# Layer 2 sampling of a four-layer convolution kernel: placings as two column tiles, convolution mid-chunk, bias by halves, far hats sent first

## The reference, cut to what matters

```
def bilinear_gather(x, py, px):
    y0, x0 = floor(py), floor(px);  wy, wx = py - y0, px - x0
    corners = [(y0, x0, (1-wy)*(1-wx)), (y0, x0+1, (1-wy)*wx), (y0+1, x0, wy*(1-wx)), (y0+1, x0+1, wy*wx)]
    return sum(x[corner] * weight * valid for each corner)            # (B, C, 9, H, W)
def deform_conv(x, offset, w, b):
    py, px = base_y + dy, base_x + dx                                 # 9 taps, own offsets per pixel
    return einsum('bckhw,ock->bohw', bilinear_gather(x, py, px), w) + b
s0 = deform_conv(x, conv3x3(x, off_w0, off_b0), dw0, db0)
s1 = deform_conv(x, conv3x3(x, off_w1, off_b1), dw1, db1)
wts = softmax(...mean of s0 and s1...);  fused = wts[0] * s0 + wts[1] * s1
return fused + conv1x1(x, cr_w, cr_b) * gate
```

## Time and profile before

| | |
|---|---|
| median of 3 runs | 1371.48 us (1370.13 to 1371.91) |
| profiled execution, its own time | 1369.67 us |
| its span in the trace | 1367.9 us |
| PE (TensorE matmul) busy | 1123.3 us, 82% of the span |
| DVE (VectorE) busy | 889.0 us, 65% |
| POOL (GpSimd) busy | 663.8 us, 49% |
| ACT (ScalarE) busy | 641.7 us, 47% |
| stage `windows1` | about 383 to 769 us |
| all spreads L1604 | x1296 matmuls, 100.6 us busy |
| all samples L1623 | x1536 matmuls, 166.3 us busy |
| all convolution matmuls L1635 | x1728, 75.7 us busy |

### The profile page before, as it was taken

The page is one execution under the profiler, slowest core; times in us unless marked ns, Lnnn a source line. Parts: engine busy times, 40 slices in busy tenths (PEclk is TensorE's granted clock), DMA queues, the critical chain, the costliest instruction groups (busy, mean ns, idle before and its releaser), DMA issues. The chain is left out here.

```text
span 1367.9 us, 31420 instructions
## 1 busy us (share of the span) xinstructions
PE 1123.3 (82%) x13256; PEld 607.0 (44%) x13256; DVE 889.0 (65%) x1220; ACT 641.7 (47%) x1096; POOL 663.8 (49%) x503
## 2 busy tenths in 40 slices
PE   3970189878749999999999487799999999998658
PEld 2440077753316666666666343233333333334323
DVE  3788945566956666666666368646666676666623
ACT  1646025353636666666666443144444444445310
POOL 2000011103336676677665430188888888888500
PEclk9985599988859999999999787699999999999769
DMA  4100000001244555555544005000000000001002
GB/s 86 23 1 0 0 3 3 2 18 36 53 129 144 145 162 163 151 148 161 163 148 133 2 1 139 1 1 2 1 2 1 2 1 2 2 10 71 1 18 71
DMA packets 41840, 75.13 MB, mean 55 GB/s; under 512 B 20876, under 2 KB 26093, under 8 KB 40925
## 3 DMA queue, kind: packets, MB, share of 16 engines
q1 hardware_dynamic: 41533, 72.77, 19.0%
q10 hardware_dynamic: 160, 0.30, 0.1%
HBM read 60.73 MB, written 9.33 MB: 51 GB/s over the span
## 5 line engine op out<-in xcount | busy, mean ns | idle before, releaser
L2246 POOL TENSOR_TENSOR arena_sb<-arena_sb 128x768 f32<-128x768 f32 x168 | 323.4, 1925 | 120.5 <-ACT arena_sb L2207 99.8
L2207 ACT ACTIVATE arena_sb<-ps 128x768 f32<-128x768 f32 x216 | 174.8, 810 | 243.4 <-PE ps L2136 241.3
L2261 DVE TENSOR_REDUCE arena_sb<-ps 128x4 f32<-128x1536 f32 x108 | 188.9, 1758 | 127.7 <-PE ps L2103 126.2
L2136 PE MATMUL ps<-arena_sb 33*64 33x384 f32 x1728 | 187.4, 502 | 11.5 <-ACT arena_sb L2207 5.5
L1623 PE MATMUL ps<-arena_sb 120*64 120x216 f32 x1536 | 166.3, 355 | 9.7 <-DVE arena_sb L1745 9.7
L2148 PE MATMUL ps<-arena_sb 64*64 64x384 f32 x1728 | 168.1, 488 | 3.4 <-ACT arena_sb L2214 3.4
L1623 PEld LDWEIGHTS ps<-arena_sb 120*64 120x64 f32 x1536 | 104.2, 136 | 61.2 <-issue 21.9
L1685 ACT ACTIVATE xp_sb<-ps 128x432 f32<-128x432 f32 x192 | 101.9, 531 | 51.2 <-PE ps L1623 47.9
L2103 PE MATMUL ps<-arena_sb 32*128 32x384 f32 x864 | 113.4, 600 | 12.6 <-DVE arena_sb L2261 6.6
L1767 POOL TENSOR_SCALAR xp_sb<-xp_sb 128x384 f32<-128x384 f32 x69 | 102.9, 1492 | 39.7 <-PE ps L1604 28.5
L1739 DVE TENSOR_TENSOR arena_sb<-ps,arena_sb 120x384 f32<-120x384 f32 x216 | 119.5, 553 | 1.1
(11 more groups left out here) (249 smaller groups left out, 1655.8 us busy)
## 6 DMA issues: line engine op xcount, KB each, us to landing
xn_sb<-far_hats SPq DMA_DIRECT2D x96, 270.0 KB
arena_sb<-far_hats SPq DMA_DIRECT2D x48, 270.0 KB
arena_sb<-pixel_major SPq DMA_DIRECT2D x96, 120.0 KB, 4.4
far_hats<-xp_sb SPq DMA_DIRECT2D x24, 162.0 KB
pixel_major<-arena_sb SPq DMA_DIRECT2D x24, 108.0 KB
x_sb<-in_x SPq DMA_DIRECT2D x4, 576.0 KB, 8.4
arena_sb<-arena_sb SPq DMA_DIRECT2D x8, 288.0 KB, 5.6
xn_sb<-in_W SPq DMA_DIRECT2D x1, 2304.0 KB, 8.9
```

The lines of the kernel that those rows point to most:

```text
L2136: mm = pe.matmul(p_scores(g)[64 * i:64 * i + 64, h, :], kp[own, key:key + 64], qp[own, PIX * b2 + CH * ib:PIX * b2 + CH * ib + CH], start= ...
L2207: act.activation(pt[g % SLOTS].rearrange("p (h n) -> p h n", h=2), p_scores(g), ACT.Exp)\
L2246: pool.tensor_tensor(acc, first, pt[g % SLOTS], ALU.add).then_inc(S["pool_added"], 1)
L2261: v.tensor_reduce(part.rearrange("p (a u j) -> p a u j", a=3, u=NB)[:, a, :, jc], p_m(m), AX.X, ALU.max)\
```

## The change

- A placing is issued as two matmuls of 64 columns each, one for each column half of the array, the form of the samples.
- The groups are rearranged: spreads 0, 1 / 2, 3 / 4 / 5, 6 / 7, 8, samples 0, 1 / 2, 3 / none / 4, 5 / 6, 7, placings (far, 0, 1, 2) in groups 0, 1, 3 and 4, always between spreads and samples. Group 2 has the convolution behind its one spread.
- The convolution in the middle of chunk n computes the upper half of chunk n and the lower half of chunk n - 1 (whose samples 4 to 7 are still there). The first computes one half, and a last one behind the last chunk the other half of chunk 23.
- The bias is split by halves: ScalarE takes the upper half of both banks, VectorE the lower half of both, each signalling after every bank. The two turns behind a convolution wait each for its own bank.
- VectorE's bias stands between weights 4 and 5 of the next chunk.
- SyncE sends the far hats of chunk 0 (store and three reloads) ahead of the windows of chunks 0 and 1.

```diff
@@ -1495,6 +1495,7 @@
     pq = [ps[:, 512 * (6 + i):512 * (6 + i) + 512] for i in range(2)]
     pc = [ps[:, 512 * (6 + v):512 * (6 + v) + CH // 2] for v in range(2)]
     S4 = smp.rearrange("p (s y x) -> p s y x", s=TAPS, y=ROWS)
+    scf = sc.rearrange("p h n -> p (h n)")
     size = SLOTS * CH // 2
     hat = [[k["xn"][:, size * (2 * i + part):size * (2 * i + part) + size].bitcast(mybir.dt.float16)
             .rearrange("p (q n) -> p q n", q=SLOTS) for part in range(2)] for i in range(2)]
@@ -1502,29 +1503,26 @@
     far = temp[0:FAR, SLOTS, :]
     far_dram = k["far"]
 
-    def steps_of(i):
-
-        return range(2 * i, min(2 * i + 2, STEPS))
-
-    def tail(n, i):
-
-        return n + 2 < NQ and i < SLOTS
-
-    def head(n, i):
-
-        return n + 2 < NQ and i == SLOTS
-
-    ORDER = (SLOTS,) + tuple(range(SLOTS))
-    turn_of = {("place", 0, q): at for at, q in enumerate(ORDER)}
+    def halves(n):
+
+        return range(0 if n < NQ else 1, 2 if n else 1)
+
+    SPREADS = ((0, 1), (2, 3), (4,), (5, 6), (7, 8))
+    SAMPLES = ((0, 1), (2, 3), (), (4, 5), (6, 7))
+    MIDDLE = 2
+    ORDER = {0: SLOTS, 1: 0, 3: 1, 4: 2}
+    turn_of = {("place", 0, q): at for at, q in enumerate(ORDER.values())}
     for n in range(-1, NQ):
         for i in range(GROUPS):
-            if head(n, i):
+            if n + 2 < NQ and i != MIDDLE:
                 turn_of["place", n + 2, ORDER[i]] = len(turn_of)
-            if n >= 0 and 2 * i < PAIRS:
-                turn_of["sample", n, 2 * i] = len(turn_of)
-                turn_of["sample", n, 2 * i + 1] = len(turn_of)
-            if tail(n, i):
-                turn_of["place", n + 2, ORDER[i]] = len(turn_of)
+            if n >= 0:
+                for j in SAMPLES[i]:
+                    turn_of["sample", n, j] = len(turn_of)
+    after_conv = {}
+    for n in range(NQ):
+        first = min(turn_of["sample", n, 4], turn_of.get(("place", n + 2, ORDER[3]), len(turn_of)))
+        after_conv[first], after_conv[first + 1] = n + 1, n + 1
 
     with nc.Block() as block:
         @block.sync
@@ -1562,11 +1560,11 @@
                     sp.dma_start(xd[blk][KW // 2 * a:KW // 2 * (a + 1), :],
                                  src.unsqueeze(0).to_broadcast([WH, IW, BLOCK * CH])).then_inc(S[f"far_in{blk}"], 16)
 
-            window(0)
-            window(1)
             far_away(0)
             for blk in range(3):
                 far_back(0, blk)
+            window(0)
+            window(1)
             for n in range(-1, NQ):
                 if n >= 1 and n + 1 < NQ:
                     window(n + 1)
@@ -1580,12 +1578,17 @@
             def empty(u):
                 if u >= 2:
                     pe.wait_ge(S["emptied"], u - 1)
+                if u in after_conv:
+                    pe.wait_ge(S[f"sc{u % 2}"], 2 * after_conv[u] - 1)
 
             def place(m, q):
                 u = turn_of["place", m, q]
                 empty(u)
-                pe.matmul(pq[u % 2][:, 0:CH], k["selp"][:, q, :], o3[:, CH * m:CH * m + CH], start=True, stop=True)\
-                    .then_inc(S["filled"], 1)
+                for h in range(2):
+                    own = slice(64 * h, 64 * h + 64)
+                    mm = pe.matmul(pq[u % 2][own, 0:CH], k["selp"][:, q, own], o3[:, CH * m:CH * m + CH],
+                                   start=True, stop=True, skip_group_check=True)
+                mm.then_inc(S["filled"], 1)
 
             def spread(m, t):
                 g = m * STEPS + t
@@ -1609,9 +1612,6 @@
                 if i == 0:
                     pe.wait_ge(S["weights"], (n + 1) * STEPS)
                     pe.wait_ge(S[f"loaded{n % 2}"], 64 * (n // 2 + 1))
-                    if n:
-                        pe.wait_ge(S["sc0"], n)
-                        pe.wait_ge(S["sc1"], n)
                 u = turn_of["sample", n, i]
                 empty(u)
                 band, pair = divmod(i, NTX // 2)
@@ -1626,32 +1626,34 @@
                 mm.then_inc(S["filled"], 1)
 
             def conv(n):
-                pe.wait_ge(S["emptied"], turn_of["sample", n, PAIRS - 1] + 1)
+                last = ("sample", n, 3) if n < NQ else ("sample", n - 1, PAIRS - 1)
+                pe.wait_ge(S["emptied"], turn_of[last] + 1)
                 for t in range(TAPS):
                     for v in range(2):
                         own = slice(64 * v, 64 * v + 64)
-                        for h in range(2):
+                        for h in halves(n):
                             at = CH * t + CH // 2 * h
                             mm = pe.matmul(pc[v][64 * h:64 * h + 64, :], k["dws"][own, t, :], smp[own, at:at + CH // 2],
                                            start=(t == 0), stop=(t == TAPS - 1), skip_group_check=True)
                 mm.then_inc(S["conv"], 1)
 
-            for q in ORDER:
+            for q in ORDER.values():
                 place(0, q)
             for n in range(-1, NQ):
                 for i in range(GROUPS):
                     if n + 1 < NQ:
-                        for t in steps_of(i):
+                        for t in SPREADS[i]:
                             spread(n + 1, t)
-                    if head(n, i):
+                    if i == MIDDLE:
+                        if n >= 0:
+                            conv(n)
+                        continue
+                    if n + 2 < NQ:
                         place(n + 2, ORDER[i])
-                    if n >= 0 and 2 * i < PAIRS:
-                        sample(n, 2 * i)
-                        sample(n, 2 * i + 1)
-                    if tail(n, i):
-                        place(n + 2, ORDER[i])
-                if n >= 0:
-                    conv(n)
+                    if n >= 0:
+                        for j in SAMPLES[i]:
+                            sample(n, j)
+            conv(NQ)
 
         @block.scalar
         def _(act):
@@ -1680,7 +1682,9 @@
                 u = turn_of["sample", n, i]
                 band, pair = divmod(i, NTX // 2)
                 act.wait_ge(S["filled"], u + 1)
-                if i == 0 and n:
+                if band and not pair:
+                    act.wait_ge(S["conv"], n + 1)
+                elif n and not pair:
                     act.wait_ge(S["conv"], n)
                 act.activation(S4[:, :, IH * band:IH * band + IH, 2 * IW * pair:2 * IW * pair + 2 * IW],
                                pq[u % 2][:, 0:TAPS * IH * 2 * IW].rearrange("p (s y x) -> p s y x", s=TAPS, y=IH), ACT.Copy)\
@@ -1688,29 +1692,26 @@
 
             def biased(n):
                 act.wait_ge(S["conv"], n + 1)
-                for h in range(2):
-                    at = CH * n + CH // 2 * h
-                    last = act.activation(sc.rearrange("p h n -> p (h n)")[0:64, at:at + CH // 2],
-                                          pc[0][64 * h:64 * h + 64, :], ACT.Identity,
-                                          bias=k["dbs"][64 * h:64 * h + 64, 1:2])
-                last.then_inc(S["sc0"], 1)
-
-            for q in ORDER:
+                for v in range(2):
+                    act.activation(scf[64 * v:64 * v + 64, CH * n:CH * n + CH // 2], pc[v][0:64, :], ACT.Identity,
+                                   bias=k["dbs"][0:64, 1 + v:2 + v]).then_inc(S[f"sc{v}"], 1)
+
+            for q in ORDER.values():
                 magnitude(0, q)
             for n in range(-1, NQ):
                 for i in range(GROUPS):
                     if n + 1 < NQ:
-                        for t in steps_of(i):
+                        for t in SPREADS[i]:
                             keep_x(n + 1, t)
-                    if head(n, i):
+                    if i == MIDDLE:
+                        if n >= 0:
+                            biased(n)
+                        continue
+                    if n + 2 < NQ:
                         magnitude(n + 2, ORDER[i])
-                    if n >= 0 and 2 * i < PAIRS:
-                        keep(n, 2 * i)
-                        keep(n, 2 * i + 1)
-                    if tail(n, i):
-                        magnitude(n + 2, ORDER[i])
-                if n >= 0:
-                    biased(n)
+                    if n >= 0:
+                        for j in SAMPLES[i]:
+                            keep(n, j)
 
         @block.vector
         def _(v_):
@@ -1740,18 +1741,18 @@
 
             def biased(n):
                 v_.wait_ge(S["conv"], n + 1)
-                for h in range(2):
-                    at = CH * n + CH // 2 * h
-                    last = v_.tensor_scalar(sc.rearrange("p h n -> p (h n)")[64:128, at:at + CH // 2],
-                                            pc[1][64 * h:64 * h + 64, :], k["dbs"][64 * h:64 * h + 64, 2:3], None, ALU.add)
-                last.then_inc(S["sc1"], 1)
+                for v in range(2):
+                    v_.tensor_scalar(scf[64 * v:64 * v + 64, CH * n - CH // 2:CH * n], pc[v][64:128, :],
```

(13 more changed lines are left out.)

## The result

The changed kernel takes 1376.25 us, the median of 6 runs (1372.66 to 1378.64), against 1370.31 for the kernel before in 6 runs (1367.71 to 1371.91), the three of the table above and three more. The ratio is 1.0046, 95% interval 1.0031 to 1.0061: slower by about 6 us. Forecast were 8.7 us more, 1380.2. The direction held, and so did the mechanism, the hold of the second sample. Two terms of the sum were off: the order of the groups costs 4.6 us and not 9.7, and the start gives back 1.6 and not 2.8. The two errors point in opposite directions and partly cancel, so the number is nearer than its terms are.

A forecast was written before the change was run, and what follows sets the result against it. TensorE's in-order stream was taken to set the pace. Order of groups +9.7, start -2.8 and end +1.8 make +8.7 us: profiled execution 1378.4, median of runs 1380.2, own range 1375 to 1385, whole range 1370 to 1387.

The forecast's parts named there:

- the hold of the second sample: After a placing, the second sample waits for ScalarE to evict the placing's bank, 1.97 us after the spreads.
- the order of the groups: Placings between spreads and samples in four groups: chunk 15.54 against 15.10 us, +0.44 for each of 22 chunks, +9.7 us.
- the start: Far hats sent first in the lead-in: first reload 3.6 us earlier, partly lost at chunk 1's reload; -2.8 us.
- The column tiles: Placing as two tiles takes 0.19 us, hidden in the gap before the held sample: cost 0, upper end 0.15 per placing.
- rival B: No change: the cheaper way from placing into samples (0.19 for 0.27) pays for most of the hold; 1373 us; 9 in 100.
- The split bias: Bias by halves behind the convolution removes the 0.39 us wait; worth up to 0.46 alone, but eaten in this kernel.
- the eviction queue: ScalarE's biases, copies and placing eviction behind the convolution: late next, at +2.33 us, making that group 3.21 us.
- VectorE and GpSimd: VectorE's later biases and weights, and GpSimd's hat slots, are each covered by 0.4 us in a chunk: no cost.
- The cover: GpSimd's slot 2 ends about 8.5 us after the convolution, the spread needing it starts at 8.91: 0.4 us spare.
- The end: Last weight made later, so GpSimd's normalization ends later; extra half convolution of about 3.1 us runs beside it; +1.8 us.
- A: Rival, faster: second sample not held, bias wait gone; rounds of 2.59, chunk 14.9, 1366 us; 13 in 100.
- C: Rival, slower still: two-tile placing takes more than the free 0.39 us, or slot 2's cover is gone; 1389 to 1393; 8 in 100.

The follow-up runs named there:

- full: The kernel after with the placing back as one matmul over 128 columns, all else as changed; ratio to before 1.0061.
- cols: The kernel before with only the placings as two column tiles, in their old places; ratio to before 0.9987.
- hats: The kernel before with only the far hats of chunk 0 sent ahead of the windows; ratio to before 1.0005.
- bias_hats: The kernel before with the bias split by halves and the far hats of chunk 0 first; ratio to before 0.9933.
- bias_hats_w: The kernel before with bias by halves, far hats first, and the windows of chunk 1 sent behind chunk 1's far hats; ratio to before 0.9897.
- all4: As bias_hats_w, with the placings also as two column tiles in their old places; ratio to before 0.991.
- ahead: The kernel after with the placings of groups 0, 1 and 4 ahead of the spreads, on TensorE and in ScalarE's evictions; ratio to before 0.998.

## Why the prediction was right, point by point

**The order of the groups (forecast +0.44 a chunk, measured +0.21).** Right in each piece but one. Group 3: 3.21 forecast, 3.21 measured. Lone spread 0.70 and convolution 3.08: the same. The three other groups: 2.85 forecast, 2.77 measured; this term was mis-sized by 0.08, three times a chunk, 5 us in all. I took the whole distance of 1.97 from today's group 3. There the spreads stand behind a placing, and ScalarE's copies start 0.65 after them, because ScalarE must first take that placing out:

```profile
538.16 0.48 ACT L1670 ACTIVATE xp_sb<-ps 128x384 f32<-128x384 f32 x1
```

In after they stand behind a sample, and the copies start 526.22 - 525.64 = 0.58 after them; the placing's eviction takes 0.50 instead of 0.53, and from copies to eviction it is 0.76 instead of 0.74. The kernel before already shows the first: the lone spread at 540.73, also behind a sample, has its copy at 541.31, 0.58 after it. I read the row of the right operation in the wrong neighbourhood. With the 0.58 alone the chunk would have been forecast at 15.33.

**The column tiles (0, upper end +0.15 a placing).** Right. From placing to sample it is 0.19 where nothing is waited for (526.43 to 526.62), the value I took, and the price is hidden: `full` has the same chunk. The Trainium skill ("TensorEngine Tiling (Array Packing)", "Key Properties") says that a change of tiling mode drains TensorE. The runs agree in kind: 0.27 to 0.29 where the shape of the tile changes behind a placing, 0.18 to 0.19 where it does not. The saving that rival B drew from it is not there: `cols` gains 0.04 a chunk and `full` loses nothing. In this kernel spreads lie on one side of a placing and samples on the other, so one of its two sides changes shape in either form.

**The split bias (worth up to 0.46, eaten by the eviction queue).** Right, and shown apart: 0.37 alone, and in after the second sample at +2.33 behind the convolution, as forecast.

**VectorE and GpSimd (no cost).** Right, narrowly. GpSimd's slot 2 ends at 530.99, 8.56 behind the convolution (8.5 forecast), and the spread that wants it starts at 531.18 without waiting. The cover was 0.4 in the forecast, and with the quicker groups it is 0.2. In chunk 22, which has no placings, the same spread does wait:

```profile
745.36 0.86 PE L1607 MATMUL ps<-xn_sb,arena_sb 32*120 32x384 f16 x12 [0.18 <-POOL xn_sb L1773]
```

**The start (-2.8).** The first half right: chunk 0's spreads come 3.4 us earlier in the stage (18.5 against 21.9). The second half was mis-sized: 1.8 of them are lost again in chunk 0, where 0.6 was forecast for the wait for chunk 1's reload.

```profile
405.87 0.56 DVE L1738 TENSOR_TENSOR arena_sb<-ps,xn_sb 120x384 f32<-120x384 f32 x1 [5.09 <-DMA xn_sb<-far_hats]
```

This weight starts 22.72 after the stage's start against 22.96 in before: earlier by 0.24; its reload goes out 17.38 after the start, in before 17.39, as the same bytes go ahead of it. Chunk 0 lasts 341.07 - 21 x 15.31 = 19.6 us against 334.65 - 21 x 15.10 = 17.6. I had priced two spreads' waits at 0.6; TensorE stands still 1.15 and 0.30 us for them (ahead of the spreads at 407.04 and 407.88). And I had left the clock out. The windows view of the kernel after, in the columns of the earlier trace rows, the granted clock being the third number from the end:

```profile
384.00:405.14 21.14, 12.94 (x88) 5.36 (x88) 12.22 (x26) 8.31 (x19) 10.64 (x11) 0.50 0.56 169
405.14:408.55 3.41, 1.97 (x24) 0.85 (x22) 2.68 (x6) 1.62 (x4) 1.04 (x1) 1.00 0.69 216
408.55:411.97 3.42, 3.42 (x24) 1.89 (x20) 1.13 (x3) 1.64 (x4) 2.32 (x3) 0.50 0.48 147
```

In before the clock rises once, at 412.41, and stays. In after it rises earlier, to 2.4 GHz, TensorE waits for the two weights, and it falls back to 1.2 GHz until 411.97. `full`, `hats` and `bias_hats`, which have the same wait, show the same fall; in `bias_hats_w` and `all4`, where TensorE waits less, it rises at 407.03 and 407.16 and stays. That the wait brings the fall is what these runs suggest; none tests it alone. From chunk 0's first spread on, before is at half the clock for 6.3 us and after for 6.9. So my estimate of the 1.8 is 1.45 for the two waits and some 0.3 for the clock, not taken apart by a run; without the fall more would have been gained. Net -1.6 where -2.8 was forecast.

**The end (+1.8).** Right: from chunk 22's spreads to the stage's end 30.8 us (742.71 to 773.47) against 28.7 (740.81 to 769.47), +2.1. The extra convolution is covered, as forecast:

```profile
756.73 16.26 POOL L1779 TENSOR_SCALAR xn_sb<-x_sb,stats_sb 128x2304 f32<-128x2304 f32 x2 [11.42 <-DVE arena_sb L1740]
...
768.33 3.14 PE L1636 MATMUL ps<-xp_sb,arena_sb 64*64 64x192 f32 x36 [0.63 <-ACT xp_sb L1689]
771.52 0.88 DVE L1745 TENSOR_SCALAR arena_sb<-ps,dbs_sb 64x192 f32<-64x192 f32 x2 [6.76 <-PE ps L1636]
```

GpSimd ends at 772.99, the last bias at 772.40. The half convolution in two quadrants takes 3.14 us, as long as the whole one in four.

**The sum in new numbers:** 22 x 0.21 = 4.6, start -1.6, end +2.1: +5.1, the stage's difference. By the runs' medians it is 5.9. The rest, 0.8, is less than what code that is alike in both kernels differed by on either side of the stage, 1.1 and 1.0 us. Part of the hit is luck: with the order's term alone put right (5.1 less) the forecast would be 1375.1, at the lower edge of my own range of 1375 to 1385; the too hopeful start covered 1.2 of the order's error.

Of the rivals, A needed the hold to be absent, and it was there in every group; B's 1373 lies 3.3 below the measured time, my 1380.2 lies 4.0 above it, so by the number B was nearer; its mechanism is excluded by `full` and `cols`. C needed over 0.39 from placing to sample: it was 0.19 in three groups. In the group behind the convolution it was 0.38 (523.22 to 523.60), but that is no price of the tiles, for `full` has 0.37 there with one matmul; the bank comes free with the biases, of which VectorE's end at 523.45 (522.57 + 0.88).

## What to carry to other kernels

Where two banks are taken in turn, ask of each product what must be evicted for the second next one, and where that eviction stands in the evicting engine's order: moving a product moves its eviction too, and `ahead` shows that the place of three placings alone, with their evictions, makes a chunk of 15.31 out of one of 14.87. Before sizing such a hold from one place in a trace, look at what the evicting engine does just before it, and compare how the same wait starts behind other neighbours. A bundle of changes is worth taking apart: here one part (the bias by halves) gained 0.5%, two gained nothing that the times can tell (the far hats first, the two tiles), and the order of the placings cost more than all gained.

## What was not expected of the hardware

Code that is the same in all these kernels took from 382.24 us (`all4`) to 387.31 (`ahead`) until the stage's start in the profiled executions, 384.24 in before and 383.15 in after. For a difference of 0.4% the repeating part (some 20 equal distances) tells more than a span. A weight that came 3.75 us earlier in `hats` was worth 0.9 us: the next transfer of its kind stood behind the same bytes of the same queue as before, and TensorE waited for it. And the granted clock, once up, went back to half in the kernels in which TensorE then waited some 1.5 to 2.1 us for weights (after, `full`, `hats`, `bias_hats`; 2.53 in `ahead`, with the same fall), but not in `bias_hats_w` and `all4`, where it waited less. An earlier start of TensorE's work is worth less than it seems where a wait follows it.
